# Adjacency of a graph layer: four slots per 32 destinations, and the destination one-hot with the edge block innermost

## The reference, cut to what matters

```
dst, src sorted by dst                                 # 20000 edges, 1250 nodes
agg0[dst[e]] += x0[src[e]]                             # layer 0: weight 1
agg1[dst[e]] += x1[src[e]] * edge_weight[e]            # layer 1
```

## Time and profile before

| | us |
|---|---|
| Median of 3 runs (2592.21 to 2596.95) | 2593.01 |
| Span of the profiled execution | 2590.1 |
| Edges stage and entry to the next (0 to the first source one-hot) | 45.7 |
| Adjacency stage, first source one-hot to the last sum on POOL | 211.6 |
| PE / DVE / POOL busy within these 211.6 us | 181.2 / 194.4 / 72.3 |

### The profile page before, as it was taken

The page is one execution under the profiler, slowest core; times in us unless marked ns, Lnnn a source line. Parts: engine busy times, 40 slices in busy tenths (PEclk is TensorE's granted clock), DMA queues, the critical chain, the costliest instruction groups (busy, mean ns, idle before and its releaser), DMA issues. The chain is left out here.

```text
span 2590.1 us, 36761 instructions
## 1 busy us (share of the span) xinstructions
PE 2365.0 (91%) x14144; PEld 2286.5 (88%) x14145; DVE 1091.0 (42%) x1852; ACT 712.6 (28%) x1213; POOL 337.5 (13%) x313
## 2 busy tenths in 40 slices
PE   3888988548889999999999999999999999999996
PEld 3888888435878999999999999999999999999996
DVE  8998344643654234242332424334242332424322
ACT  0333523324532222222222222222222222222221
POOL 3333100111001011101110111011101110111101
PEclk9898999668988999999999999999999999999998
DMA  1000010215012011010200201011020110102001
GB/s 63 0 0 0 1 65 1 90 28 183 26 40 70 17 49 59 17 66 4 72 33 33 76 1 65 26 51 57 9 76 13 53 59 17 66 1 75 33 1 40
DMA packets 73330, 105.83 MB, mean 41 GB/s; under 512 B 7219, under 2 KB 42499, under 8 KB 73211
## 3 DMA queue, kind: packets, MB, share of 16 engines
q1 hardware_dynamic: 68731, 100.37, 11.3%
q0 software_dynamic: 4480, 3.64, 0.5%
HBM read 95.08 MB, written 10.40 MB: 41 GB/s over the span
## 5 line engine op out<-in xcount | busy, mean ns | idle before, releaser
L1547 DVE TENSOR_TENSOR hidden_lo<-gelu,hidden_hi 128x416 fp32r<-128x416 f32 (+1 forms) x384 | 247.6, 645 | 1151.4 <-ACT hidden_hi L1615 1151.4
L1611 ACT ACTIVATE gelu<-psum,b1cols 128x416 f32<-128x416 f32 (+1 forms) x384 | 233.8, 609 | 1253.5 <-PE psum L494 1253.4
L492 PE MATMUL psum<-hidden_hi,w_hi 128*128 128x416 f32 (+1 forms) x1536 | 543.2, 354 | 12.7 <-issue 11.4
L492 PE MATMUL psum<-f_xT_hi,w_hi 128*128 128x416 f32 (+1 forms) x1536 | 543.4, 354 | 0.2 <-ACTq L1603 0.2
L494 PE MATMUL psum<-hidden_hi,w_lo 128*128 128x416 f32 (+1 forms) x1536 | 542.7, 353 | 0.0
L493 PE MATMUL psum<-f_xT_lo,w_hi 128*128 128x416 f32 (+1 forms) x1536 | 541.7, 353 | 0.0
L494 PE MATMUL psum<-f_xT_hi,w_lo 128*128 128x416 f32 (+1 forms) x1536 | 541.1, 352 | 0.0
L493 PE MATMUL psum<-hidden_lo,w_hi 128*128 128x416 f32 (+1 forms) x1536 | 540.0, 352 | 0.0
L1594 POOL TENSOR_TENSOR acc<-acc,y_scaled 128x416 f32<-128x416 f32 (+1 forms) x192 | 198.9, 1067 | 1562.4 <-DVE y_scaled L1538 1562.4
L492 PEld LDWEIGHTS psum<-hidden_hi,w_hi 128*128 128x128 f32 x1536 | 289.7, 189 | 18.7 <-issue 16.2
L492 PEld LDWEIGHTS psum<-f_xT_hi,w_hi 128*128 128x128 f32 x1536 | 290.2, 189 | 4.9 <-issue 1.7
(11 more groups left out here) (280 smaller groups left out, 2059.6 us busy)
## 6 DMA issues: line engine op xcount, KB each, us to landing
w_raw<-in_w SPq DMA_DIRECT2D x128, 512.0 KB, 4.1
expert_raw<-in_experts SPq DMA_DIRECT2D x8, 1024.0 KB, 5.7
leaf_all<-leaf_rows SPq DMA_DIRECT2D x8, 625.0 KB, 4.9
rows_by_place_d<-zero_rows SPq DMA_DIRECT2D x1, 2560.0 KB, 16.6
rows_by_place<-rows_by_place_d SPq DMA_DIRECT2D x5, 512.0 KB, 6.5
expert_results_d<-expert_results SPq DMA_DIRECT2D x16, 160.0 KB, 5.0
x_rows<-in_x SPq DMA_DIRECT2D x1, 2500.0 KB
out_rows<-x_rows SPq DMA_DIRECT2D x10, 250.0 KB
```

The costliest lines, as they stand in the source:

```text
L492: t.matmul(out, stat[0], mov[0], start=start, stop=False)
L1547: v.tensor_tensor(hlo[:, s % 4, 0:w], G[:, s % 3, 0:w], hhi[:, s % 4, 0:w].bitcast(F32), ALU.subtract).then_inc(lo_cut, 1)
L1611: a.activation(G[:, s % 3, 0:w], g.psum[:, 4 + s % 4, 0:w], ACT.Gelu, bias=g.b1cols[:, bass.ds(e * 16 + half * 8 + 2 * q + j, 1)]).then_in ...
```

## The change

SLOTS goes from 6 to 4. The loops over groups are unrolled in the program text: window numbers are constants now, and DVE's and PE's bounds of the next group are read at the end of a group. `rkey` and its waits are gone: the one-hot instruction itself adds 2048 x window to the node numbers and compares with the key, whose column is chosen by a register; padding keys are -5000. `bn_stats` comes after the second window of a group. `D_all` is [125, 4, 32, block]: its four instructions run over 160 blocks innermost, in bf16, all on DVE, and compare against `row_of`, a table that POOL fills with 32 memsets. A matmul takes from it 128 columns that lie NB + SLOTS = 164 elements, 328 bytes, apart.

```diff
-SLOTS = 6
+SLOTS = 4
@@ phase_edges
-    rem = room("rem", [EB, NB], F32)
-    parts = room("parts", [EB, NB, 3], BF16)
+    parts = room("parts", [EB, 3, NB], BF16)
+    rem16 = room("rem16", [EB, NB], BF16)
+    row_of = room("row_of", [EB, WIN, NB], BF16)
...
-            s.mark(v.memset(g.key[:, :], -1.0))
-            s.mark(v.memset(g.D_all[:, NB:NB + SLOTS, :, :], 0.0))
+            s.mark(v.memset(g.key[:, :], -5000.0))
+            s.mark(v.memset(g.D_all[:, :, :, NB:NB + SLOTS], 0.0))
...
-            d, shape = g.D_all[:, 0:NB, :, :], [EB, NB, WIN]
-            s.then(v.tensor_tensor(d[:, :, 0, :], rem[:, :].unsqueeze(2).to_broadcast(shape),
-                                   g.iota32[0:EB, :].unsqueeze(1).to_broadcast(shape), ALU.is_equal))
-            v.sem_inc(one_hot, 1)
-            weighted_rows(v, s.mark, 0, NB_V)
+            d, shape = g.D_all[:, :, :, 0:NB], [EB, WIN, NB]
+            v.wait_ge(numbered, WIN)
+            s.then(v.tensor_tensor(d[:, 0], rem16[:, :].unsqueeze(1).to_broadcast(shape), row_of[:, :, :], ALU.is_equal))
+            for c in range(3):
+                s.mark(v.tensor_tensor(d[:, 1 + c], d[:, 0], parts[:, c, :].unsqueeze(1).to_broadcast(shape), ALU.mult))
...
         def _(q):
-            q.wait_ge(one_hot, 1)
-            weighted_rows(q, lambda ins: ins.then_inc(one_hot, 1), NB_V, NB)
+            for w in range(WIN):
+                q.memset(row_of[:, w, :], float(w)).then_inc(numbered, 1)
@@ phase_adjacency, DVE
+            bounds = group_bounds(v, regs[0], 0)
+            for w in range(NW):
+                i, j = divmod(w, GROUP)
+                lo, hi = bounds[j]
+                for p in range(PAIRS):
+                    v.wait_ge(used, w * PAIRS + p + 1)
+                    for u in (2 * p, 2 * p + 1):
+                        ins = v.tensor_scalar(S[:, u, :], g.i10[:, :], float(KEY * w),
+                                              g.key[:, bass.ds(lo + u, 1)], ALU.add, ALU.is_equal)
+                    ins.then_inc(made, 1)
+                with v.Fori(lo + SLOTS, hi) as b:
+                    v.wait_ge(more_used, v.snap(n))
+                    v.tensor_scalar(S_more[:, :], g.i10[:, :], float(KEY * w), g.key[:, bass.ds(b, 1)],
+                                    ALU.add, ALU.is_equal).then_inc(more_made, 1)
+                    v.reg_add(n, n, 1)
+                if j == 1:
+                    v.bn_stats(g.stats[:, i, :], g.x_rows[:, i, :]).then_inc(stat, 1)
+                if j == GROUP - 1 and w + 1 < NW:
+                    bounds = group_bounds(v, regs[(i + 1) % 2], i + 1)
@@ phase_adjacency, PE (the loop over windows as above; the further block likewise)
-                                               g.D_flat[:, bass.ds((lo + u) * 128, 128)],
+                                           g.D_flat[:, :, bass.ds(lo + u, 1)],
@@ gnn_ffn_kernel
-        g.D_all = room("dst_onehot", [EB, NB + SLOTS, 4, WIN], BF16)
-        g.D_flat = g.D_all[:, :, :, :].rearrange("p b a w -> p (b a w)")
+        g.D_all = room("dst_onehot", [EB, 4, WIN, NB + SLOTS], BF16)
+        g.D_flat = g.D_all[:, :, :, :].rearrange("p a w b -> p (a w) b")
```

More of the change, by code:

```diff
@@ L183, in phase_edges @@
     later_loaded = sem("e_later_loaded")
-    one_hot = sem("e_one_hot")
     turned = sem("e_turned")
@@ L205, in phase_edges @@
     ]
[L207 to L213, removed]
+    numbered = sem("e_numbered")
     with nc.Block() as block:
@@ L247, in _ @@
             s.mark(v.tensor_copy(halves(g.key[:, 0:NB]), table[:, 0]))
-            s.mark(v.tensor_copy(halves(rem[:, :]), table[:, 1]))
+            s.mark(v.tensor_copy(halves(rem16[:, :]), table[:, 1]))
             s.then(v.tensor_copy(halves(wcol[:, :]), table[:, 2]))
[L251 to L255, removed]
+            s.then(v.tensor_copy(parts[:, 0, :], wcol[:, :]))
+            s.then(v.tensor_tensor(wres[:, :], wcol[:, :], parts[:, 0, :], ALU.subtract))
+            s.then(v.tensor_copy(parts[:, 1, :], wres[:, :]))
+            s.then(v.tensor_tensor(wres2[:, :], wres[:, :], parts[:, 1, :], ALU.subtract))
+            s.then(v.tensor_copy(parts[:, 2, :], wres2[:, :]))
             v.wait_ge(turned, 2)
@@ L319, in phase_adjacency @@
     S = room("src_onehot", [EB, SLOTS, NC], BF16)
-    rkey = room("rkey", [EB, GROUP, SLOTS], F32)
     S_more = room("src_onehot_more", [EB, NC], BF16)
-    rkey_more = room("rkey_more", [EB, 1], F32)
     WP = room("weight_parts", [128, 2, NT, 3, WIN], F32)
@@ L325, in phase_adjacency @@
     PAIRS = SLOTS // 2
-    keyed = sem("a_keyed")
     made = sem("a_made")
     used = sem("a_used")
-    more_keyed = sem("a_more_keyed")
     more_made = sem("a_more_made")
@@ L343, in group_bounds @@
     def group_bounds(eng, regs, i):
-        eng.load(regs, g.bounds[0:1, bass.ds(i * (2 * GROUP), 2 * GROUP)])
+        eng.load(regs, g.bounds[0:1, i * 2 * GROUP:(i + 1) * 2 * GROUP])
         return [(eng.snap(regs[2 * j], min_val=0, max_val=NB - 1), eng.snap(regs[2 * j + 1], min_val=1, max_val=NB))
@@ L351, in _ @@
         def _(v):
-            regs = [v.alloc_register(f"v_bound{i}") for i in range(2 * GROUP)]
+            regs = [[v.alloc_register(f"v_bound{k}_{i}") for i in range(2 * GROUP)] for k in range(2)]
             n = v.alloc_register("more_made_blocks")
@@ L355, in _ @@
             v.wait_ge(g.x_loaded, 16)
[L356 to L381, removed]
@@ L387, in _ @@
             t.sem_inc(drained, 2)
-            regs = [t.alloc_register(f"t_bound{i}") for i in range(2 * GROUP)]
+            regs = [[t.alloc_register(f"t_bound{k}_{i}") for i in range(2 * GROUP)] for k in range(2)]
             n = t.alloc_register("more_used_blocks")
             t.reg_mov(n, 1)
[L391 to L401, removed]
-                                               g.D_flat[:, bass.ds((lo + u) * 128, 128)],
[L403 to L406, removed]
-                        for c in range(NT):
[L408 to L414, removed]
@@ new lines, in _ @@
+            bounds = group_bounds(t, regs[0], 0)
+            for w in range(NW):
+                i, j = divmod(w, GROUP)
+                lo, hi = bounds[j]
+                ps = banks(w % 2)
+                t.wait_ge(drained, w + 1)
+                for p in range(PAIRS):
+                    t.wait_ge(made, w * PAIRS + p + 1)
+                    for u in (2 * p, 2 * p + 1):
+                        for c in range(NT):
+                            ins = t.matmul(ps[:, c * 128:(c + 1) * 128], S[:, u, c * 128:(c + 1) * 128],
+                                           g.D_flat[:, :, bass.ds(lo + u, 1)],
+                                           start=u == 0 and c % 4 == 0, stop=False, skip_group_check=True)
+                    ins.then_inc(used, 1)
+                with t.Fori(lo + SLOTS, hi) as b:
+                    t.wait_ge(more_made, t.snap(n))
+                    for c in range(NT):
+                        ins = t.matmul(ps[:, c * 128:(c + 1) * 128], S_more[:, c * 128:(c + 1) * 128],
+                                       g.D_flat[:, :, bass.ds(b, 1)],
+                                       start=False, stop=False, skip_group_check=True)
+                    ins.then_inc(more_used, 1)
+                    t.reg_add(n, n, 1)
+                t.matmul(ps[:, 0:128], g.zeros[0:EB, :], g.zeros[0:EB, :], start=False, stop=True,
+                         skip_group_check=True).then_inc(summed, 1)
+                if j == GROUP - 1 and w + 1 < NW:
+                    bounds = group_bounds(t, regs[(i + 1) % 2], i + 1)
@@ L416, in _ @@
         @block.scalar
         def _(a):
[L418 to L426, removed]
+            for w in range(NW):
+                par = w % 2
+                ps = banks(par).rearrange("p (c a w) -> p c a w", c=NT, a=4)
+                a.wait_ge(summed, w + 1)
+                a.wait_ge(parts_free, w + 1)
+                a.activation(WP[:, par], ps[:, :, 1:4, :], ACT.Copy).then_inc(copied, 1)
+                a.activation(g.A0T[:, :, w * WIN:(w + 1) * WIN], ps[:, :, 0, :], ACT.Copy).then_inc(drained, 1)
@@ L430, in _ @@
             q.sem_inc(parts_free, 2)
[L431 to L440, removed]
+            for w in range(NW):
+                par = w % 2
+                q.wait_ge(copied, w + 1)
+                q.wait_ge(parts_free, w + 2)
+                q.tensor_tensor(T[:, :, :], WP[:, par, :, 0, :], WP[:, par, :, 1, :],
+                                ALU.add).then_inc(added, 1)
+                q.wait_ge(added, w + 1)
+                q.tensor_tensor(g.A1T[:, :, w * WIN:(w + 1) * WIN], T[:, :, :], WP[:, par, :, 2, :],
+                                ALU.add).then_inc(parts_free, 1)
 class NormSteps:
```

## The result

The changed kernel takes 2868.35 us (median, 2867.54 to 2870.03) against 2593.24 for the kernel before beside it: ratio 1.106, 95% interval 1.104 to 1.107. The profiled spans are 2865.7 and 2590.1. Forecast were 2601 us in a range of 2535 to 2850; the time lies above the range, 20 us beyond rival C.

A forecast was written before the change was run, and what follows sets the result against it. DVE was taken as the bound, PE close behind. The adjacency stage would start 14.5 us earlier and, with PE then the bound, end 7.7 later: span 2597.8, with 2.9 added 2601 us; range 2535 to 2850.

The forecast's parts named there:

- rival C: Adjacency matmuls: each step costs PE what it costs DVE, 0.231 us a matmul, 2848 us; chance 0.26 (all above 0.118).
- What bounds the kernel now: Adjacency stage before the change: DVE bounds it, busy 194.4 of 211.6 us, with PE not far behind at 181.2.
- Destination one-hot: Start of the adjacency stage: four DVE instructions at 3.1 us each; first source one-hot at 31.2, 14.5 us earlier.
- the load of x: Before the first source one-hot: x lands at about 30.5 us and is the next thing late if instructions are cheaper.
- Blocks per window: Adjacency windows: 204 blocks in place of 280, 5.1 per window; four windows loop twice, about 0.7 us idle PE each.
- DVE per window: DVE in the adjacency stage: 4.10 us a window, 172 us in all with double rounds and bound loads.
- rival A: Adjacency matmuls: the steps cost nothing, or less than DVE hides; DVE stays the bound, 2543 us; chance 0.30.
- The matmuls: Adjacency matmuls with stepped operand: 0.110 us each, 229.6 us in all, so PE becomes the bound.
- The numbers: Chances of the whole forecast: forecast 0.38, A 0.30, B (between A and forecast) 0.06, C 0.26; range 2535 to 2850.
- The sign: Whole kernel: faster with chance 0.41, slower 0.51, within 0.2% (5 us) 0.08.
- Program text: PE's and DVE's unrolled code of 40 windows, read once: counted as nothing; at 0.056 us a matmul it could show.

The follow-up runs named there:

- e10: Changed kernel with a contiguous one-hot built by DVE alone and one of POOL's two additions per window left out (third weight part missing): 2512.53 us.
- e1: Changed kernel with the destination one-hot laid out and built as before (128 columns in a row, DVE and POOL): 2533.07 us, ratio 0.978 to before.
- e8: Changed kernel with the destination one-hot laid out and built as before, and six slots instead of four: 2570.43 us.
- e9: Changed kernel with the one-hot in runs of 4 adjacent elements and POOL's table filled by 16 memsets of 4-byte words: 2521.27 us, ratio 0.972.
- e3: Changed kernel with each window's matmuls reading from a fixed place in steps of 1 to 164 elements (sums wrong): 0.056 to 0.320 us a matmul.
- e4: Changed kernel with matmuls reading runs of 1 to 128 adjacent elements with jumps between (sums wrong): runs of 2 cost 0.120 us a matmul.
- e2: Kernel before with only the destination one-hot's new layout and its building added, six slots kept: 3084.84 us.
- e7: Changed kernel with only the pitch between columns padded from 328 to 384 bytes: 2824.90 us.

## Why the prediction was wrong, point by point

**What bounds the kernel now.** Right: DVE, with POOL in its way, PE close behind. e10 bears out the second part.

**Destination one-hot.** Right in its end: first source one-hot forecast at 31.2, measured 31.95. The instructions took 2.81 where I took 3.1; the estimate of 2.7 by the Trainium skill, "VectorE: DVE Perf Modes", section "The perf-mode tier table", was nearer. DVE was ready at 27.94 and then stood 4.01 us: the load of x was late next, as said. It did not land late, though: from 30 to 31 us 27 GB/s moved where 128 had moved before, so its last bytes came at some 30.2. What I had too short was the way from there to the first one-hot, 1.7 us where I had allowed 0.7.

**Blocks per window.** Right: 44 runs of the further block, 440 matmuls, four waits of up to 0.8 us.

**DVE per window.** It was never the bound, so this term decided nothing, but it sized rival A. e1 shows it too dear: 172/40 = 4.3 us a window with double rounds and loads, where e1's sums end 3.70 us apart (the first at 50.46, the last at 194.78). 0.37 of the 0.6 is POOL's share: I carried 1.53 us over from the kernel before; in e1 the same two additions take 1.15 - 0.55 from L364 and 2.53 - 1.97 from L359, 1.16 us. It isn't the number of one-hots: e8 has seven, and loses 1.15 - 0.55 and 3.46 - 2.90 (six one-hots at 0.55 + 5 x 0.47), 1.16 again. What cost the kernel before 0.37 more is open. With 3.70 rival A comes to 2519; e9 measured 2521.

**The matmuls.** This step failed. I set the equal bytes per ns of 2- and 4-byte columns against the 1.8 ns per element that DVE's rows gave, called the first nearer because it was PE's own, and took 0.110 us. The runs show 0.240. Both rows read their operand in order, at 4.6 to 4.7 bytes a ns; they say nothing on how many bytes one access brings, and e3 has 0.057 us at a step of two elements, where pieces of 4 bytes would give 0.11. What an access costs stood only in the rows with a step: 0.231 from L953 and L958, 4% from the truth, on another engine and at a pitch of 32 bytes, where PE itself takes 0.232 in e3. In order, eight columns share a piece's 1.8 ns (8 x 0.44 = 3.5 ns) and it hides. PE being faster than DVE in order made it no faster in steps. That both engines pay one price of the memory is my reading, not shown: DVE's figure is pieced together from two instructions (0.74 + 1.07 ns), and no run varied DVE's step, so part of so close a match may be luck. The rule of the Trainium skill, "SBUF — State Buffer", section "Door 1: The DMA port swizzle", that each further line costs, spoke for the same side, and I gave it no weight for want of a number. Its other half, that two hits in a line bring full rate, e3 doesn't bear out for PE's moving operand: a step of 4 elements has two in each line and costs 0.115 us, twice the price in order.

**The numbers.** C had 0.26 and a point of 2848, and I closed the range 2 us above that point, as if C had no width of its own. Its sum lacked 0.009 us a matmul, 18 us, for the pitch. The sign had 0.51 for slower, and that held, but half of the 0.51 rested on the price of the forecast, which did not.

**Program text.** Rightly counted as nothing: even in e1, with matmuls 0.056 us apart, the unrolled code doesn't show.

## What to carry to other kernels

Lay an operand out for whoever reads it most: the one-hot is built by 4 instructions and read by 2040 matmuls, and 12 us won in the building (the first one-hot at 31.95 where e1 has 44.24) cost 345 in the reading (e1's span is 333 shorter all the same). If another order makes the building cheap, keep the innermost run at 8 aligned bytes; that gave both. To price an access pattern that the trace doesn't have on this engine, look for any engine that reads with such a step, and give its price real weight: here it came within 4%. That is one case, not a rule.

## What the runs showed of the hardware that I had not expected

- A moving operand of 2-byte elements costs 1.8 ns per 16-byte piece touched, hidden up to 32 pieces per 128 columns: steps of 2 elements are free (0.057 us), 3 cost 0.088, 8 cost 0.226. Runs of 8 off multiples of 8 bytes are the exception, 0.070 to 0.073.
- Far pitches differ: 0.217 us at multiples of 64 bytes, 0.240 at 328, 0.253 at 332, 0.320 at 96. Padding 328 to 384 bytes alone won 43 us.
- In e3 the granted clock fell to 0.50 at 57.0 us, when PE had been busy without a gap since 41.5 with steps of 3 to 5 elements, and it stayed there for 420 us of a PE that was busy 99%. In e4 it was 0.50 from some 194.7 to 238 us, beginning 5 us after single elements at a step of 8 had followed windows with runs. In the changed kernel and in e2 and e7, with stepped operands from the first matmul on, it stayed at 1.00. What brought the one and the other about I did not test.
- Two-input instructions of DVE and POOL side by side took turns by whole instructions, and the waits stand in the profile as longer durations: 6.71 us for 3.35 us of DVE's work.
